# Sums of folded blocks on VectorE, sums of x on GpSimd in one stretch, and corrections of two tiles added in PSUM

## The reference

```python
def _L0_cond_ref(x, adapter_indices, W, lora_A, lora_B):
    base_out = jnp.einsum('bsi,io->bso', x, W)
    xr = jnp.einsum('bsi,bir->bsr', x, lora_A[adapter_indices])
    return base_out + jnp.einsum('bsr,bro->bso', xr, lora_B[adapter_indices])

def _L0_ffn_ref(x, W_base, b_base, W_gate, A, B):       # 8 experts, rank 16, top 2
    result = jnp.einsum('bnd,od->bno', x, W_base) + b_base
    probs = jax.nn.softmax(jnp.einsum('bnd,ed->bne', x, W_gate), axis=-1)
    top_p, top_i = jax.lax.top_k(probs, 2)
    top_p = top_p / jnp.sum(top_p, axis=-1, keepdims=True)
    route_w = jnp.sum(jax.nn.one_hot(top_i, 8) * top_p[..., None], axis=-2)
    hw = jnp.einsum('bnd,erd->bner', x, A) * route_w[..., None]
    return result + jnp.einsum('bner,eor->bno', hw, B)

out = x + _L0_ffn_ref(_L0_cond_ref(x, itok, W, lora_A, lora_B), W_base, b_base, W_gate, A, B)
```

## Time and profile before

| | us |
|---|---|
| runs | 71.29, 71.37, 72.53 (median 71.37) |
| profiled execution, its own time | 71.1 |
| its span (first to last instruction) | 69.9 |
| PE, PEld busy | 60.4 (86%), 57.9 (83%) |
| DVE busy | 52.2 (75%) |
| ACT busy | 35.3 (50%) |
| POOL busy | 31.6 (45%) |
| granted TensorE clock, mean | 0.998 of full speed |
| waits of PE after the first 20 us: on `hw` (one wait) | 2.4 |
| on the low part of `hw` (two waits) | 2.2 |
| on the copy of `xa_t` | 1.0 |
| on the copy of a left bank | 0.3 |

### The profile page before, as it was taken

The page is one execution under the profiler, slowest core; times in us unless marked ns, Lnnn a source line. Parts: engine busy times, 40 slices in busy tenths (PEclk is TensorE's granted clock), DMA queues, the critical chain, the costliest instruction groups (busy, mean ns, idle before and its releaser), DMA issues.

```text
span 69.9 us, 1331 instructions
## 1 busy us (share of the span) xinstructions
PE 60.4 (86%) x406; PEld 57.9 (83%) x406; DVE 52.2 (75%) x146; ACT 35.3 (50%) x94; POOL 31.6 (45%) x54
## 2 busy tenths in 40 slices
...
GB/s 0 271 328 362 379 381 341 59 9 325 233 328 26 82 127 64 61 65 71 65 64 61 76 9 5 248 52 0 0 0 175 128 7 0 0 0 175 125 48 252
DMA packets 5528, 8.74 MB, mean 125 GB/s; under 512 B 1009, under 2 KB 2065, under 8 KB 5522
## 3 DMA queue, kind: packets, MB, share of 16 engines
...
q0 software_dynamic: 256, 0.52, 2.2%
q10 hardware_dynamic: 288, 0.27, 1.1%
...
## 4 chain that ended last, share of the span: by engine, by line
PE 52%; DVE 20%; ACT 9%; POOL 7%; DMA 4%; issue 4%; DVEq 0%; POOLq 0%
PE bank L817 11%; PE bank L819 10%; PE bank L818 10%; PE bank L825 7%; PE bank L827 5%; DMA w_raw<-fold_in 4%; DVE route L753 3%; DVE onehot L747 3%; DVE weighted L751 3%; PE bank L937 2%; POOL x_raw L370 2%; PE bank L985 2%; ACT w_raw L473 2%; POOL x_mix_first L368 2%; DVE x_lo L629 2%
## 5 line engine op out<-in xcount | busy, mean ns | idle before, releaser
L817 PE MATMUL bank<-c_hi,x_hi 128*128 128x408 f32 (+1 forms) x40 | 13.6, 341 | 0.3 <-ACT w_raw L548 0.3
L819 PE MATMUL bank<-c_hi,x_lo 128*128 128x408 f32 (+1 forms) x40 | 13.4, 334 | 0.0
L818 PE MATMUL bank<-c_lo,x_hi 128*128 128x408 f32 (+1 forms) x40 | 13.4, 334 | 0.0
L817 PEld LDWEIGHTS bank<-c_hi,x_hi 128*128 128x128 f32 x40 | 7.5, 188 | 0.8 <-ACT w_raw L548 0.6
L629 DVE TENSOR_TENSOR x_lo<-x_raw,x_hi 128x512 fp32r<-128x512 f32 (+1 forms) x9 | 7.5, 847 | 0.7 <-ACT x_hi L459 0.6
L819 PEld LDWEIGHTS bank<-c_hi,x_lo 128*128 128x128 f32 x40 | 7.5, 188 | 0.0
L818 PEld LDWEIGHTS bank<-c_lo,x_hi 128*128 128x128 f32 x40 | 7.5, 188 | 0.0
L334 POOL DMA_DIRECT2D lora_raw<-lora x8 | 4.4, 554 | 6.5 <-issue 6.3
L414 POOL TENSOR_TENSOR x_raw<-x_raw 128x256 f32<-128x256 f32 x2 | 1.8, 890 | 10.0 <-DVE x_raw L710 10.0
L954 PE MATMUL bank<-ident,hw 128*128 128x128 f32 x8 | 2.3, 286 | 4.6 <-DVE hw L756 2.4
L537 ACT ACTIVATE top_exp<-top_diff 128x2 f32<-128x2 f32 x8 | 1.6, 204 | 8.7 <-DVE top_diff L744 8.7
...
## 6 DMA issues: line engine op xcount, KB each, us to landing
...
bw_rows<-bw_hi SPq DMA_DIRECT2D x16, 40.5 KB, 2.0
...
bw_rows<-bw_lo SPq DMA_DIRECT2D x8, 40.5 KB, 2.0
...
```

Source lines behind the costliest of these rows:

```text
L817: nc.tensor.matmul(out, a_hi, b_hi, start=first, stop=False, skip_group_check=True)
L818: nc.tensor.matmul(out, a_hi, b_lo, start=False, stop=False, skip_group_check=True)
L819: return nc.tensor.matmul(out, a_lo, b_hi, start=False, stop=last, skip_group_check=True)
```

## The change

VectorE now forms the sums of the folded blocks itself, each with one operand in PSUM and one in SBUF: `x3_raw`, SUM6 and SUM1 as one instruction of 512 columns each, `x4_raw` and SUM7 as two each (392 and 256 columns). ScalarE copies only three pieces to SBUF for that (the left columns of row blocks 0 and 1, `raw_c01`, and B22, `raw_b22`) where it copied all of them. The sums of x of pairs 2 and 3 stand one behind the other in GpSimd's order, ahead of the adapters' columns of tiles 2 and 3; their buffers are moved so that they wait for two and for four split tiles. `sum_e` and `sum_u2` go to VectorE. For tiles 4 and 5 the corrections are written by VectorE into the tiles' PSUM banks (`seed_u`), and the products `M7(2)` and `M6(2)` add to what is there; `add_u` and its two semaphore waits on SyncE are gone. For tiles 6 and 7 both corrections are formed after `split_hw(7)` (`sum_u`). Some splits move to other places in the orders of ScalarE and VectorE. The computed values are the same sums.

```diff
-        x_mix_first = sb("x_mix_first", [P, 3, 2 * P])
...
-        x4_raw = part(w_flat, 2 * D, 2, LEFT)
-        raw_left = part(w_flat, 4 * D, KC, LEFT)
-        sum1_raw = part(w_flat, NT * D, 2, HALF)
-        raw_right = part(x_flat, 0, KC, HALF)
-        cs_raw = {SUM1: sum1_raw, SUM6: raw_right[:, 0:2], SUM7: raw_right[:, 2:4]}
-        x_mix = (x_mix_first[:], part(x_flat, 2 * D, 3, 2 * P))
+        x4_raw = part(w_flat, 2 * HALF, 2, LEFT)
+        raw_c01 = part(w_flat, 3 * D, 2, LEFT)
+        raw_b22 = part(w_flat, 5 * D, 2, HALF)
+        cs_raw = [part(w_flat, at * D, 2, HALF) for at in (NT, 6, 7)]
+        x_mix = [part(x_flat, 2 * k * D, 3, 2 * P) for k in range(2)]
...
-                pool.wait_ge(x_lo_done, 4)
...
+                pool.wait_ge(x_lo_done, 2 * k + 2)
...
-            def sum_c():
...
-                nc.gpsimd.tensor_tensor(sum1_raw, b11, b22, ALU.add).then_inc(cs_summed, 1)
-                pool.wait_ge(cs_summed, 1)
-                pool.wait_ge(x3_summed, 1)
-                nc.gpsimd.tensor_tensor(b22, b21, b22, ALU.add).then_inc(cs_summed, 1)
-                nc.gpsimd.tensor_tensor(b12, b11, b12, ALU.add).then_inc(cs_summed, 1)
...
-            def add_u(q):
-                k = SEVEN.index(q)
-                a, b = 2 * q, 2 * q + 1
...
             pool.wait_ge(lora_loaded, NT * DMA)
             split_la(0)
             split_la(1)
-            pool.wait_ge(bw_summed, 1)
             sum_x(2)
+            sum_x(3)
             split_la(2)
             split_la(3)
-            sum_c()
             split_la_pair(2)
-            sum_x(3)
             split_la_pair(3)
-            sum_e(2)
-            sum_u2(2)
-            sum_e(3)
-            add_u(2)
-            sum_u2(3)
...
-            copy_left_raw(0)
-            copy_left_raw(1)
+            copy_c01_raw(0)
+            copy_c01_raw(1)
             act.wait_ge(cr_summed, 2)
...
-            copy_left_raw(2)
-            copy_left_raw(3)
             split_x(2)
+            copy_b22_raw()
             act.wait_ge(bw_summed, 1)
...
             split_x(3)
-            copy_right_raw(0)
-            copy_right_raw(1)
...
             act.wait_ge(x_loaded[4], DMA)
             act.wait_ge(x_loaded[5], DMA)
             split_x_outer(2)
-            split_x_inner(2)
+            act.wait_ge(x4_summed, 2)
+            nc.scalar.copy(c_hi[:, X4, :, LORA_LEFT], x4_raw).then_inc(x4_hi_done, 1)
...
             copy_xa_t(0)
+            split_x_inner(2)
             exp_top(0)
             exp_top(1)
             act.wait_ge(x4_lo_done, 1)
             nc.scalar.mul(c_lo[:, X3, :, A_GH], c_lo[:, X4, :, GH_COLS].bitcast(F32), -1.0).then_inc(x3_gh_done, 1)
             split_hw(0)
-            split_cs(SUM1, 1)
+            split_cs(SUM1, 2)
+            split_hw(1)
             split_xd(2)
-            split_hw(1)
...
-            dve.wait_ge(left_raw_done, KC)
-            nc.vector.tensor_tensor(x4_raw, raw_left[:, 2:4], raw_left[:, 0:2], ALU.subtract).then_inc(x4_summed, 1)
+            b12, b22 = (bank[4 + n][:].rearrange("p (c n) -> p c n", c=2) for n in range(2))
+            b11 = raw_c01[:, :, GH:]
+            dve.wait_ge(b22_raw_done, 1)
+            nc.vector.tensor_tensor(x3_raw, b12, raw_b22, ALU.subtract).then_inc(x3_summed, 1)
+            dve.wait_ge(c01_raw_done, 2)
+            nc.vector.tensor_tensor(cs_raw[SUM6], b12, b11, ALU.add).then_inc(cs_summed, 1)
             dve.wait_ge(bw_hi_done, 1)
             lo(bw_lo[:, HALF:], bwl_bank[:, 0:LEFT], bw_hi[:, HALF:], bw_lo_done)
             dve.wait_ge(bw_hi_done, 2)
             lo(bw_lo[:, 0:HALF], bwr_bank[:, 0:HALF], bw_hi[:, 0:HALF], bw_lo_done)
+            nc.vector.tensor_tensor(cs_raw[SUM1], b22, b11, ALU.add).then_inc(cs_summed, 1)
             split_x(3)
+            for n in (1, 0):
+                nc.vector.tensor_tensor(x4_raw[:, n], bank[2 + n][:, 0:LEFT], raw_c01[:, n], ALU.subtract).then_inc(x4_summed, 1)
+                nc.vector.tensor_tensor(cs_raw[SUM7][:, n], bank[2 + n][:, GH:LEFT], raw_b22[:, n], ALU.add).then_inc(cs_summed, 1)
...
+            def seed_u(q):
+                k = SEVEN.index(q)
+                dve.wait_ge(e_done, k + 1)
+                dve.wait_ge(m1_done, k + 1)
+                dve.wait_ge(yr_done, 2 * q - 1)
+                nc.vector.tensor_tensor(right(2 * q), first_bank[:, M1_COLS], mix(q)[:, 0], ALU.add).then_inc(u1_done, 1)
+                dve.wait_ge(u1_done, k + 1)
+                dve.wait_ge(z_done, k + 1)
+                dve.wait_ge(yr_done, 2 * q)
+                nc.vector.tensor_tensor(right(2 * q + 1), right(2 * q), mix(q)[:, 2], ALU.add).then_inc(u2_done, 1)
...
             split_xa(0)
-            dve.wait_ge(right_raw_done, 2)
-            nc.vector.tensor_tensor(x3_raw, raw_right[:, 0:2], raw_right[:, 2:4], ALU.subtract).then_inc(x3_summed, 1)
-            dve.wait_ge(x4_hi_done, 1)
-            lo(c_lo[:, X4, :, LORA_LEFT], x4_raw, c_hi[:, X4, :, LORA_LEFT], x4_lo_done)
             split_xa(1)
             dve.wait_ge(x3_hi_done, 1)
             lo(c_lo[:, X3, :, A_RIGHT], x3_raw, c_hi[:, X3, :, A_RIGHT], x3_lo_done)
+            dve.wait_ge(x4_hi_done, 1)
+            lo(c_lo[:, X4, :, LORA_LEFT], x4_raw, c_hi[:, X4, :, LORA_LEFT], x4_lo_done)
             split_x_outer(2)
-            split_x_inner(2)
 
             gate(0)
             gate(1)
+            split_x_inner(2)
             split_xa(2)
             split_hw(0)
             split_xa(3)
...
 
             gate(2)
             gate(3)
+            sum_e(2)
             split_xa(4)
             split_hw(2)
             split_xa(5)
             split_hw(3)
             sum_z(2)
-            split_xd(2)
-            split_cs(SUM7, 2)
             split_x_outer(3)
             split_x_inner(3)
+            split_xd(2)
 
             gate(4)
             gate(5)
-            sum_u1(2)
+            seed_u(2)
+            split_cs(SUM7, 2)
             split_cs(SUM6, 3)
+            sum_e(3)
             split_xa(6)
             split_hw(4)
             split_xa(7)
...
             split_xd(3)
 
             gate(6)
-            sum_u1(3)
             gate(7)
             split_hw(6)
             split_hw(7)
+            sum_u(3)
...
-                if t < 3:
-                    pe.wait_ge(left_raw_done, t + 1)
+                if t < 2:
+                    pe.wait_ge(c01_raw_done, t + 1)
+                if t == 2:
+                    pe.wait_ge(cs_summed, 4)
...
-            def seven_right(out, q, which, done):
+            def seven_right(out, q, which, done, seeded):
...
-                                 cs_hi[:, which, c, :], cs_lo[:, which, c, :], c == 0, False)
+                                 cs_hi[:, which, c, :], cs_lo[:, which, c, :], c == 0 and not seeded, False)
                 return mm
 
             def M1(q):
-                seven_right(first_bank[:, M1_COLS], q, SUM1, 1).then_inc(m1_done, 1)
+                seven_right(first_bank[:, M1_COLS], q, SUM1, 1, False).then_inc(m1_done, 1)
 
             def M7(q):
+                if q == SEVEN[0]:
+                    pe.wait_ge(u2_done, 1)
                 pe.wait_ge(yr_done, 2 * q - 1)
-                seven_right(right(2 * q), q, SUM7, 2)
+                seven_right(right(2 * q), q, SUM7, 2, q == SEVEN[0])
 
             def M6(q):
                 pe.wait_ge(yr_done, 2 * q)
-                seven_right(right(2 * q + 1), q, SUM6, 3)
+                seven_right(right(2 * q + 1), q, SUM6, 3, q == SEVEN[0])
...
-                    pe.wait_ge(left_raw_done, KC)
+                    pe.wait_ge(cs_summed, 3)
```

More of the change, by code:

```diff
@@ L158, in adaln_ffn_kernel @@
         cs_summed, cs_hi_done, cs_lo_done = sem("cs_summed"), sem("cs_hi_done"), sem("cs_lo_done")
-        x_summed, x_mixed, xd_hi_done, xd_lo_done = sem("x_summed"), sem("x_mixed"), sem("xd_hi_done"), sem("xd_lo_done")
+        x_summed = [sem(f"x_summed{k}") for k in range(len(SEVEN))]
+        x_mixed = [sem(f"x_mixed{k}") for k in range(len(SEVEN))]
+        xd_hi_done, xd_lo_done = sem("xd_hi_done"), sem("xd_lo_done")
         la_diff_done = sem("la_diff_done")
@@ L469, in scalar_program, with copy_c01_raw, copy_b22_raw @@
             nc.scalar.copy(ffn_b_hi[:], ffn_b_raw[:]).then_inc(ffn_b_hi_done, 1)
[L471 removed]
+            def copy_c01_raw(i):
                 act.wait_ge(cl_lo_done, i + 1)
[L473 to L477 removed]
+                nc.scalar.copy(raw_c01[:, i], bank[i][:, 0:LEFT]).then_inc(c01_raw_done, 1)
+            def copy_b22_raw():
+                act.wait_ge(cr_lo_done, 2)
+                nc.scalar.copy(raw_b22[:], bank[5][:].rearrange("p (c n) -> p c n", c=2)).then_inc(b22_raw_done, 1)
             for i in range(KC):
@@ L516, in split_cs @@
                 nc.scalar.copy(cs_hi[:, which], cs_raw[which]).then_inc(cs_hi_done, 1)
-            act.wait_ge(x4_summed, 1)
-            nc.scalar.copy(c_hi[:, X4, :, LORA_LEFT], x4_raw).then_inc(x4_hi_done, 1)
             act.wait_ge(x3_summed, 1)
```

(16 more changed lines are left out.)

50 lines of the change are left out of this document (13 added, 37 removed).

## The result

The changed kernel takes 68.46 us (median of 68.0 to 68.52, 4 runs) against 71.34 for the kernel before beside it (71.29 to 72.53): ratio 0.958, 95% interval 0.953 to 0.964, so faster by 4%. Ratios leave out executions more than 1.5% above the fastest of their kernel, and so need not be those of the medians. The forecast was 67.3, its range 66.2 to 69.2. The profiled execution took 68.5, its span 67.3.

A forecast was written before the change was run, and what follows sets the result against it. The prediction took the time to be lost in TensorE's gaps, three of four ending on a late VectorE. Its terms, 3.85 - 1.0 + 1.1 - 0.15 = 3.8 off 71.1, gave 67.3 us, range 66.2 to 69.2.

The forecast's parts named there:

- (a): From the folded sums to T2(1): gate(0) no longer held by GpSimd, TensorE's gaps close; gain 3.85 us (3.4 to 4.3).
- (b): VectorE behind gate(5): second seed, a split and sum_e(3) delay T2(5); cost 1.0 us (0.7 to 1.3).
- (c): Gates 6 and 7: two steps no longer held by GpSimd, sum_u1(3) gone from between; gain 1.1 us (0.7 to 1.43).
- (d): End: two sums of sum_u stand before VectorE's last additions; cost 0.15 us (0 to 0.3).
- The second: Sums out of PSUM before T1(0) are held by GpSimd like those in SBUF; 3.0 us slower, 74.1; chance 0.05.
- The first: The collision moves with GpSimd's sums of x, up to gate(0); 1.3 us lost, 68.6, or 69.7; chance 0.17.
- The third: VectorE's longer list after 40 us reaches the path; gain only 1.4 us, so 69.7; chance 0.08.

The follow-up runs named there:

- sums_back_beside_gate: The changed kernel with three unused GpSimd sums of 512 columns added behind split_la(3), beside the first gates: 71.49 us, ratio 0.988 to the kernel before.
- splits_early: The changed kernel with VectorE's two splits of cs_lo (SUM7, SUM6) moved from behind the seeds to ahead of them: 67.14 us.
- tail_between: The changed kernel with the two late sums of pair 3 (sum_u) moved from behind split_hw(7) to between split_hw(6) and split_hw(7): 68.36 us.
- padded: The changed kernel with 16 tiny one-column fills of a scratch buffer added to VectorE's program: 68.29 us, ratio 0.957 to the kernel before.
- end_restored: The changed kernel with sum_u(3) between split_hw(6) and split_hw(7) and 32 tiny fills in VectorE's program: 67.63 us, ratio 0.949 to the kernel before.
- columns_first: The changed kernel with GpSimd's split_la(2) moved between the sums of x of pair 2 and those of pair 3: 68.83 us.

## Why the prediction was right, and which term was not

| step | forecast | measured, from the two profiles |
|---|---|---|
| (a) to `T2(1)` | +3.85 (3.4 to 4.3) | 39.99 - 36.23 = +3.76 |
| (b) before `T2(5)` | -1.0 (0.7 to 1.3) | 57.81 - 55.13 = 2.68, so -1.08 |
| from there to `Lora_left(3)` | 0 | 59.46 - 56.98 = 2.48, so -0.20 |
| (c) gates 6 and 7 | +1.1 (0.7 to 1.43) | 65.56 - 61.94 = 3.62, so +1.14 |
| (d) end | -0.15 (0 to 0.3) | 69.9 - 67.3 = 2.6, so -1.02 |
| sum | 3.8 | 2.6 |

Of the 1.2 us by which the sum was too high, 0.87 is (d) and 0.20 the stretch that I had at zero; (a), (b) and (c) make up the rest.

**(a)** was right in mechanism: steps of 0.16 to 0.17 in `gate(0)`, no gap before `T2(0)`, `Left(2)` behind `split_la(2)`. `sums_back_beside_gate` shows the mechanism. That the size fits to 0.09 is partly luck: `Left(2)` came at 31.59 against a forecast 31.2, but `T2(0)` followed it after 2.31 and `T2(1)` after 2.33 more, where I had taken 2.40 and 2.56 from the kernel before. What I had not seen is that copy order alone is worth 1.2 us of the time: I took the three held steps for `gate(0)`'s own, but each GpSimd sum holds whichever step meets it, and a gate that starts 0.4 earlier hands two of them to the next gate.

**(b)** was right, in place, cause and size; `splits_early` takes it back. The 0.20 behind it I had at zero: when `T2(5)` must wait, the product behind it starts 0.24 after it (55.13, 55.37), where 0.03 is usual (57.81 and 57.84 before).

**(c)** was right in place and size: the two held steps now take 0.16 and 0.18. Two small errors cancelled. A third step, `top_diff` of `gate(7)`, had been held too (0.44, now 0.23), and `sum_u1(3)` stood in the way for 0.33, not 0.42, since the next step began before its end (62.70 and 63.03). No run takes (c) back alone, so its cause rests on these rows.

**(d) failed.** I priced the last addition, and that one came as priced: it ended 0.70 after the start of the last matmul, 0.45 before, and ScalarE's store is issued then too. I did not price the addition ahead of it, for which the store of tile 6 waits: with `sum_u` in front that store was issued 0.45 after the start of the last matmul, before it was 0.13 ahead. And I had no term for VectorE's program, nine counted instructions longer by the pages (155, before 146; no row gives the 13 of my expectation), of which a piece is now transferred beside the last stores. `tail_between` and `padded` each took one away and gained little; `end_restored` took both and gave the 1 us back. Its 67.63 is near my 67.3: with the end as I had priced it, the forecast would have been about right. Why a transfer of 0.01 MB goes with landings up to 1.1 us later is not shown.

**Rivals.** The second (sums out of PSUM held) fell: 0.68 beside GpSimd sums. By the rule of the Trainium skill (SBUF — State Buffer, section Who interferes with whom) on VectorE instructions with at most one SBUF input it had to, and these rows agree for long instructions too. The first came in part: `sum_x(3)` held `c_lo`, and `columns_first` shows how 0.5 us more of GpSimd undoes a gain. The third fell: of VectorE's added instructions only those before `T2(5)`, and the two at the end, reached the path.
